# A two-layer graph network: the order of VectorE's and ScalarE's work within one turn of layer 1

## The chip, the cores and the metric

The kernel runs on one core of a Trainium2 chip. The metric is the time of one execution in microseconds of device time. The time before is 8842.36 us, the median of three runs (8837.32 to 8854.7).

## The reference, cut to what matters

12500 nodes have 64 features each; 400000 edges (src, dst) are sorted by dst. Two layers, each with a residual and a layer norm around it. Layer 0 passes every edge's pair of nodes through two small dense layers and sums over dst. Layer 1, to which the change belongs, is a graph attention with four heads:

```
x = (meta_x @ W).reshape(N, HEADS, DIM)
a_src = jnp.sum(x * att_src, axis=-1)
a_dst = jnp.sum(x * att_dst, axis=-1)
logits = leaky_relu(a_src[src] + a_dst[dst], 0.2)       # with a loop edge for each node
seg_max = segment_max(logits, dst)
ex = exp(logits - seg_max[dst])
alpha = ex / (segment_sum(ex, dst) + 1e-16)
msg = x[src] * alpha[:, :, None]
out = segment_sum(msg, dst).mean(axis=1) + bias
```

## The kernel before, in words

Edges are taken in groups of 1024 (8 tiles of 128; an edge is a partition). 8 groups are a superstep; there are 392 groups in 49 supersteps. Nodes lie in 98 blocks of 128. As edges are sorted by dst, a group touches one or two neighbouring blocks. A *turn* works on one group and one block; there are 392 + 97 = 489 turns in a layer. Every engine runs the same two nested loops (`steps`, line 250): over the groups of a superstep, and within one over the blocks of the group, the range of which it loads from a table `Bt` (line 256). Around them, `supers` goes over the supersteps; the start of one takes VectorE through `maxima` (lines 618 to 656), which makes a running maximum of the logits per node with scans.

GpSimd gathers the rows of the source nodes (64 features, a one and the four `a_src`) from DRAM into `big`, one DMA for each 128 edges, into two halves of a superstep each. It waits until the turns that read the old rows have written their Y (semaphore `y1`).

A turn is a pipeline over up to four turns. `k.has(n)` and `k.after(stage, n)` speak of the turn n before the present one. For turn t in layer 1:

- VectorE makes `rel` (dst less the block's first node, line 482) and from it `S`, the one-hot of 1024 edges x 128 nodes in bf16 (line 485). Both are in `onehot`, line 480.
- TensorE transposes S (line 970), ScalarE copies the transposes to `ST` (line 1174), TensorE looks up `a_dst` of the edges with it (line 979, stage `ad`).
- In the next turn, VectorE sums up the lookup (`adx`, 692), adds it to the logits and to the maxima (`zz`, 704 and 705), takes the leaky relu (`lz`, 713) and the difference (`dw`, 722). ScalarE takes the exp into the weights `wb` (line 1178, stage `w`).
- In the turn after, VectorE multiplies the gathered rows by the weights into `Y`, in two halves of 4 tiles (`weigh`, line 665, stages `y0` and `y1`). ScalarE copies in the last columns of Y and an f32 copy of S, `Sf`, half by half (`ends`, lines 1148 and 1149, stages `sf0` and `sf1`). TensorE sums Y over the edges of each node (`sums`, line 956, stages `U0` and `U1`) into one of two banks of `pu`. Its own order in a turn is: sums of half 0, transposes, sums of half 1, lookup. The half-0 sums wait for `tm` of the turn that used the bank before.
- One turn later, VectorE makes the new maximum of the nodes in small steps (`nz`, 700, to `dd`, 728 and 729). ScalarE takes the exp of dd into `ee` (1161), copies the maximum (1163), and makes `Tm`, the new sums scaled, in four steps (1167). VectorE scales the accumulator by ee (stage `old`, line 739), and in the following turn adds Tm to it (stage `acc`, line 684).

The order of each engine's work is written by hand. VectorE's in a turn is: Y half 0, acc, adx with the small chains zz to dw and nz to dd woven into each other, rel, S, Y half 1, old. ScalarE's is: ends of half 1, ee, Tm, ends of half 0, ST, exp of the weights. The end of a turn holds `push`, which shifts registers with the places of earlier turns (line 208). Semaphores carry every dependence.

Of the kernel before, what the change touches and what calls it, by code (L numbers as in the profile page):

```python
# [24 lines left out]
P = 128  # L25
NB = -(-N // P)
LAST = N - (NB - 1) * P
TG = 8
# [30 lines left out]
def build(nc, x, src, dst, W1, b1, W2, b2, W, att_src, att_dst, bias, out, q_dram, x_dram, srcT_dram,  # L59
# [5 lines left out]
    with ctx:  # L65
# [3 lines left out]
        def sem(name):  # L69
# [98 lines left out]
                 "az1": 0, "h0": 1, "h1": 1, "htp": 1, "hts": 1, "z2": 1, "az2": 1,  # L168
                 "h2": 2, "hi": 2, "rest": 2, "mid": 2, "lo": 3, "U": 3, "us": 4, "acc": 4},
                {"rel": 0, "S": 0, "stp": 0, "sts": 0, "ad": 0, "adx": 1, "zz": 1,  # L170
                 "lz": 1, "dw": 1, "w": 1, "sf0": 1, "sf1": 2, "y0": 2, "y1": 2, "U0": 2, "U1": 2, "nz": 3,
                 "nl": 3, "np": 3, "mnew": 3, "dd": 3, "e": 3, "mb": 3, "tm": 3, "old": 3, "acc": 4}]
        L = [{n: sem(f"l{l}_{n}") for n in LAGS[l]} for l in range(2)]

        class Turn:
# [216 lines left out]
        def _(dve):  # L392
# [3 lines left out]
            def link(ins):  # L396

                count[0] += 1
                ins.then_inc(vch, 1)
                dve.wait_ge(vch, count[0])  # L400
# [76 lines left out]
            def hv(ap, h):  # L477
                return ap[:, h * 4:(h + 1) * 4, :]

            def onehot(k, half, buf):  # L480
                k.after("S", 1)
                v.tensor_scalar(rel[:, :], dstc[:, half, ds(k.r * TG, TG)], blk[:, ds(k.b, 1)], None,  # L482
                                ALU.subtract).then_inc(L[k.l]["rel"], 1)
                k.after("rel", 0)
                v.tensor_tensor(S[:, ds(buf, TG), :], iotas[k.l][:, :].unsqueeze(1).to_broadcast([P, TG, P]),  # L485
                                rel[:, :].unsqueeze(2).to_broadcast([P, TG, P]),
                                ALU.is_equal).then_inc(L[k.l]["S"], 1)
# [4 lines left out]
            def turn0(half):  # L492
                m = L[0]

                def turn(k):
                    if k.has(4):
                        k.after("U", 4)
                        k.after("acc", 5)
                        v.tensor_reduce(usum[:, :], ps[6][:, 0:BF].rearrange("p (k d) -> p d k", k=3),
                                        AX.X, ALU.add).then_inc(m["us"], 1)  # L500
                    if k.has(3):
                        k.after("mid", 3)
                        v.tensor_tensor(h2p[:, 2, :], h2, h2p[:, 1, :], ALU.subtract).then_inc(m["lo"], 1)
                    if k.has(0):
                        onehot(k, half, (k.sn % 4) * TG)
                    elif k.has(3):
                        k.after("lo", 3)
                    if k.has(4):
                        b = blocks.back(4 - max(k.tail, 0))
                        k.after("us", 4)  # L510
                        v.tensor_tensor(x0[:, ds(b, 1), :], x0[:, ds(b, 1), :], usum[:, :].unsqueeze(1),
                                        ALU.add).then_inc(m["acc"], 1)
                    if k.has(1):
                        for h in range(2):
                            k.after(f"az{h}", 1)
                            v.tensor_tensor(hv(h1, h), ps[4 + h][:, 0:256].rearrange("p (t d) -> p t d", d=D),
                                            hv(az1, h), ALU.max).then_inc(m[f"h{h}"], 1)
                    if k.has(2):
                        k.after("az2", 2)
                        v.tensor_tensor(h2, ps[7][:, :], az2, ALU.max).then_inc(m["h2"], 1)  # L520
                        k.after("hi", 2)
                        v.tensor_tensor(h2, h2, h2p[:, 0, :], ALU.subtract).then_inc(m["rest"], 1)  # L522
                    if k.has(0):
                        blocks.push(k.b)
                return turn
# [84 lines left out]
            link(v.memset(warm[:, :], 0.0))  # L610
            link(v.memset(wb[:, :, :], 0.0))
            link(v.memset(Tm[:, :, :], 0.0))
            prime(dve, 1, "rel S adx zz lz dw y0 y1 nz nl np mnew dd old acc")
            dve.sem_inc(clean, 1)

# [54 lines left out]
            def turn1(half):  # L670
                m = L[1]

                def turn(k):
                    t = max(k.tail, 0)
                    if k.has(2):
                        at = tiles.back(2 - t)
                        k.after("w", 2)
                        weigh(k, 0, at)
                    if k.has(4):

                        ab = acc[:, ds(blocks1.back(4 - t), 1), :, :].rearrange("p b h d -> p (b h) d")
                        k.after("old", 4)
                        k.after("tm", 4)
                        v.tensor_tensor(ab, ab, Tm[:, :, :], ALU.add).then_inc(m["acc"], 1)  # L684

                    if k.has(1):
                        here = tiles.back(1)
                        zf = zz[:, :, :, :].rearrange("p a t h -> p (a t h)")  # L690
                        k.after("ad", 1)
                        v.tensor_reduce(adx[:, :, :],
                                        ps[2][:, 0:TG * 3 * H].rearrange("p (t k h) -> p t h k", k=3, h=H),
                                        AX.X, ALU.add).then_inc(m["adx"], 1)
                    if k.has(3):
                        b = blocks1.back(3 - t)
                        mb = Mx[:, ds(b, 1), :]
                        ends = pu[:, ds(((k.sn + 1) % 2) * 512, YW)]
                        k.after("U1", 3)
                        v.tensor_tensor(nz[:, 0:1, :], ends[:, UW:UW + H].unsqueeze(1), adst[:, ds(b, 1), :],  # L700
                                        ALU.add).then_inc(m["nz"], 1)
# [26 lines left out]
                        v.tensor_tensor(dd[:, 0:1, :], mb, mnew[:, :].unsqueeze(1), ALU.subtract)  # L728
                        v.tensor_tensor(dd[:, 1, :], nz[:, 2, :], mnew[:, :], ALU.subtract).then_inc(m["dd"], 1)  # L729

                    if k.has(0):
                        k.after("sf1", 2)
                        onehot(k, half, (k.sn % 2) * TG)
                    if k.has(2):
                        weigh(k, 1, at)
                    if k.has(3):
                        ab = acc[:, ds(b, 1), :, :].rearrange("p b h d -> p (b h) d")
                        k.after("e", 3)
                        v.tensor_tensor(ab, ab, ee[:, 0, :].unsqueeze(2).to_broadcast([P, H, D + 1]), ALU.mult
                                        ).then_inc(m["old"], 1)  # L740
                    if k.has(0):
                        tiles.push(k.r * TG + half * TS)
                        blocks1.push(k.b)
# [272 lines left out]
        def _(act):  # L1016
# [121 lines left out]
                    a_.copy(xT[c % 2][:, us[0] * P:(us[-1] + 1) * P], ps[4 + h][:, 0:len(us) * P]  # L1138
                            ).then_inc(tab1["tc"], 1)

            act_tiles = Past(act, "act_tile", 2, 2 * TS - TG)
            act_blocks = Past(act, "act_block", 3, NB - 1)

            def ends(k, h, back):

                k.after(f"U{h}", back + 1)
                at = act_tiles.back(back - max(k.tail, 0))
                a_.copy(Y[:, h * 4:h * 4 + 4, UW:YW], edgeE[:, ds(at + h * 4, 4), :])
                a_.copy(Sf[:, h * 4:h * 4 + 4, :], S[:, ds(((k.sn + back) % 2) * TG + 4 * h, 4), :]  # L1149
                        ).then_inc(L[1][f"sf{h}"], 1)  # L1150

            def turn1(half):
                m = L[1]

                def turn(k):
                    if k.has(2):
                        ends(k, 1, 2)
                    if k.has(3):

                        k.after("dd", 3)  # L1160
                        a_.activation(ee[:, :, :], dd[:, :, :], ACT.Exp).then_inc(m["e"], 1)  # L1161
                        b = act_blocks.back(3 - max(k.tail, 0))
                        a_.copy(Mx[:, ds(b, 1), :], mnew[:, :].unsqueeze(1)).then_inc(m["mb"], 1)
                    if k.has(3):
                        k.after("e", 3)
                        for h in range(H):
                            a = a_.activation(Tm[:, h, :], pu[:, ds(((k.sn + 1) % 2) * 512 + h * (D + 1), D + 1)],
                                              ACT.Copy, scale=ee[:, 1, h:h + 1])
                        a.then_inc(m["tm"], 1)
                    if k.has(1):  # L1170
                        ends(k, 0, 1)
                    if k.has(0):
                        k.after("stp", 0)
                        a_.copy(ST[:, :, :], ps[0][:, :].bitcast(bf16).rearrange("p (t n) -> p t n", t=TG)  # L1174
                                ).then_inc(m["sts"], 1)
                    if k.has(1):
                        k.after("y1", 2)
                        a_.activation(wb[:, :, :], dw[:, :, :], ACT.Exp).then_inc(m["w"], 1)  # L1178
                    if k.has(0):
                        act_tiles.push(k.r * TG + half * TS)  # L1180
                        act_blocks.push(k.b)
                return turn
# [53 lines left out]
```

## Time and profile before

| | |
|---|---|
| median of three runs | 8842.36 us |
| the profiled execution | 8853.59 us, span 8851.8 us |
| granted TensorE clock, mean | 0.888 |
| VectorE busy | 5775.0 us, 65% |
| GpSimd busy | 6098.9 us, 69% |
| TensorE busy (matmul) | 5979.6 us, 68% |
| ScalarE busy | 3918.0 us, 44% |

Layer 0 fills the span to about 3.9 ms, layer 1 from about 4.3 to 8.7 ms. From 4500 to 8500 us VectorE is busy 3075.88 of 4000 us, GpSimd 2816.14, TensorE 2600.49 and ScalarE 1720.59. An engine's busy time leaves out what its sequencer does by itself: register work, branches, waits. "issue" as the end of an idle time means that the engine waited for nothing that the profile shows.

### The profile page before, as it was taken

The numbers are of one execution on the slowest core, as the hardware profiler recorded it, in microseconds if no ns is written. First come the engines' busy times: TensorE is split into PE (matmuls) and PEld (weight loads), VectorE is DVE, ScalarE is ACT, GpSimd is POOL, SyncE is SP. The second block draws the span as 40 slices with busy tenths as digits, with TensorE's granted clock in tenths as the row PEclk, the third lists the DMA queues.
The fourth block names the chain that finished last, engine by engine and source line by source line (L and its number), as shares of the span: only waits on it lengthen the run. The fifth ranks groups of instructions, "written<-read, shape, count | busy, mean of one in ns | idle before, by whom it ended". The sixth has DMA issues, their size and how long they took to land.

```text
span 8851.8 us, 202989 instructions
## 1 busy us (share of the span) xinstructions
PE 5979.6 (68%) x46823; PEld 4612.0 (52%) x46824; DVE 5775.0 (65%) x13889; ACT 3918.0 (44%) x10077; POOL 6098.9 (69%) x6281
## 2 busy tenths in 40 slices
PE   4777777777777777776366666666666666666667
PEld 3556555555555555555244445444444444444446
DVE  3555555555555555556477777777777777777776
ACT  3445444544444444444244444444444444444443
POOL 4777777777777777772777776767676766766650
PEclk7889888988988888888698989999898989999897
DMA  3111111111111111112111111111111111111110
GB/s 99 40 40 40 39 40 40 40 40 40 39 40 40 40 40 40 40 40 30 27 29 30 28 28 26 28 27 28 27 27 27 27 28 26 27 28 27 27 21 15
DMA packets 276883, 301.80 MB, mean 34 GB/s; under 512 B 169511, under 2 KB 173108, under 8 KB 276566
## 3 DMA queue, kind: packets, MB, share of 16 engines
q0 software_dynamic: 200704, 265.33, 14.7%
q1 hardware_dynamic: 74082, 32.92, 1.5%
q10 hardware_dynamic: 2068, 3.20, 0.1%
q8 instruction: 13, 0.21, 0.0%
q14 instruction: 16, 0.13, 0.0%
HBM read 286.33 MB, written 16.30 MB: 34 GB/s over the span
## 4 chain that ended last, share of the span: by engine, by line
DVE 25%; issue 22%; POOL 21%; PE 18%; DVEq 6%; ACT 4%; ACTq 2%; POOLq 1%; DMA 1%; SPq 0%
POOL big L382 21%; DVE S L485 8%; PE ps L970 6%; PE pu L956 4%; DVE state L684 2%; DVE rel L482 2%; PE ps L846 2%; DVE rowA L633 1%; DVE rowD L638 1%; POOLq L373 1%; DVE Y L665 1%; DVEq L256 1%; DVEq L700 1%; ACT rowX L1087 1%; ACT ST L1174 1%
## 5 line engine op out<-in xcount | busy, mean ns | idle before, releaser
L382 POOL DMA_INDIRECT big<-x_dram,idx x3136 | 3084.8, 984 | 1442.5 <-issue 892.7
L382 POOL DMA_INDIRECT big<-q_dram,idx x3136 | 3013.0, 961 | 1041.2 <-issue 1033.9
L956 PE MATMUL pu<-Y,S 128*128 128x265 f32 x7856 | 2147.5, 418 | 738.2 <-DVE Y L665 732.5
L956 PEld LDWEIGHTS pu<-Y,S 128*128 128x128 f32 x7856 | 1497.5, 201 | 1030.8 <-issue 782.2
L665 DVE TENSOR_TENSOR Y<-big,ps 128x1040 f32<-128x1040 f32 x982 | 1210.7, 1233 | 659.0 <-ACT ps L1178 572.5
L485 DVE TENSOR_TENSOR S<-ps,rel 128x1024 f32 x978 | 1197.8, 1225 | 222.1 <-DVE rel L482 222.1
L1075 ACT COPY ST<-ps 128x512 bf16<-128x512 bf16 x978 | 538.8, 586 | 1703.7 <-PE ps L846 1703.6
L860 PE MATMUL pu<-rowX,S 128*128 128x192 bf16 x3936 | 578.0, 264 | 980.4 <-issue 718.6
L522 DVE TENSOR_TENSOR Y<-Y,rowX 128x512 f32<-128x512 f32 x491 | 341.7, 696 | 1221.3 <-ACT rowX L1087 1218.9
L860 PEld LDWEIGHTS pu<-rowX,S 128*128 x3936 | 383.7, 98 | 1174.7 <-issue 1063.5
L970 PE MATMUL ps<-identb,S 128*128 128x128 bf16 x3912 | 550.3, 231 | 523.9 <-DVE S L485 522.7
L970 PEld LDWEIGHTS ps<-identb,S 128*128 x3912 | 375.6, 96 | 838.3 <-issue 727.2
L1161 ACT ACTIVATE ee<-dd 128x8 f32<-128x8 f32 x492 | 102.6, 209 | 1412.6 <-DVE dd L729 1412.6
L1174 ACT COPY ST<-ps 128x1024 bf16<-128x1024 bf16 x489 | 494.9, 1012 | 515.0 <-PE ps L970 511.6
L846 PE MATMUL ps<-identb,S 128*128 128x128 bf16 x3912 | 551.3, 234 | 159.5 <-DVE S L485 152.8
L1149 ACT CAST S<-S 128x512 f32 x981 | 617.4, 629 | 14.1
L883 PE MATMUL ps<-state,ST 128*128 x11736 | 570.3, 199 | 0.0
L893 PE MATMUL pu<-edgeE,rowA 128*128 128x128 f32 x3920 | 567.6, 288 | 0.8 <-ACT rowA L1090 0.8
L883 PEld LDWEIGHTS ps<-state,ST 128*128 128x128 bf16 x11736 | 537.5, 102 | 45.4
L846 PEld LDWEIGHTS ps<-identb,S 128*128 x3912 | 376.0, 97 | 344.3 <-issue 235.9
L893 PEld LDWEIGHTS pu<-edgeE,rowA 128*128 128x128 f32 x3920 | 474.3, 191 | 113.3 <-issue 112.2
L878 PE MATMUL ps<-big,identb 128*128 x2934 | 529.8, 294 | 0.0
(176 smaller groups left out, 8322.6 us busy)
## 6 DMA issues: line engine op xcount, KB each, us to landing
big<-q_dram,idx POOLq DMA_INDIRECT x3136
big<-x_dram,idx POOLq DMA_INDIRECT x3136
rowD<-dst_dram SPq DMA_DIRECT2D x196, 32.0 KB
x_dram<-big SPq DMA_DIRECT2D x7, 483.0 KB, 6.1
idx<-srcT_dram SPq DMA_DIRECT2D x98, 32.0 KB, 1.7
dstc<-dstT_dram SPq DMA_DIRECT2D x98, 32.0 KB
q_dram<-state SPq DMA_DIRECT2D x2, 1536.0 KB, 9.6
out<-big SPq DMA_DIRECT2D x6, 448.0 KB
```

The lines of the kernel that those rows point to most:

```text
L382: nc.gpsimd.indirect_dma_start(o, None, x_dram if l else q_dram, bass.IndirectOffsetOnAxis(ap=idx[:, half, t:t + 1], axis=0)).then_inc(gat ...
L485: v.tensor_tensor(S[:, ds(buf, TG), :], iotas[k.l][:, :].unsqueeze(1).to_broadcast([P, TG, P]), rel[:, :].unsqueeze(2).to_broadcast([P, TG ...
L665: v.tensor_tensor(Y[:, rows, 0:UW].rearrange("p t (h d) -> p t h d", h=H), g1[:, ds(at + h * 4, 4), 0:D + 1].unsqueeze(2).to_broadcast([P, ...
L846: last = t_.transpose(o[:, t * P:t * P + P], hot[:, h * 4 + t, :], identb[:, :])
L860: last = t_.matmul(ps[6][:, 0:BF].rearrange("p (k d) -> p k d", k=3), hot[:, t, :], h2p[:, :, t * D:t * D + D], start=(t == 0), stop=(t == ...
L883: last = t_.matmul(ps[4 + h][:, t * D:t * D + D], ST[:, h * 4 + t, :], pq[:, 0, ds(k.b, 1), j, :], start=False, stop=(t == 3 and j == 2), ...
L893: last = t_.matmul(ps[7][:, j * P:j * P + P], h1T[:, j, :], w2d[:, :], start=False, stop=(j == 3), skip_group_check=True)
L956: last = t_.matmul(bank, Sf[:, t, :], Y[:, t, :], start=(t == 0), stop=(t == 7))
L970: last = t_.transpose(o[:, t * P:t * P + P], hot[:, t, :], identb[:, :])
L1075: a_.copy(ST[:, h * 4:h * 4 + 4, :], ps[h][:, 0:2 * P].bitcast(bf16).rearrange("p (t n) -> p t n", t=4)).then_inc(L[k.l][f"sts{h}"], 1)
L1149: a_.copy(Sf[:, h * 4:h * 4 + 4, :], S[:, ds(((k.sn + back) % 2) * TG + 4 * h, 4), :]).then_inc(L[1][f"sf{h}"], 1)
L1174: a_.copy(ST[:, :, :], ps[0][:, :].bitcast(bf16).rearrange("p (t n) -> p t n", t=TG)).then_inc(m["sts"], 1)
```

## The change

VectorE's turn in layer 1 is put in another order: rel, Y half 0, S, Y half 1, old, adx, acc, then the woven small chains. `onehot` is split into `places` (rel) and `onehot` (S). The scaling of the accumulator (`old`) goes one turn later, so that it stands in the same turn as acc, two instructions ahead of it. ScalarE's turn is put in the order: ends of half 0, ST, exp of the weights, ends of half 1 (now for the turn one back and not two), ee, the copy of the maximum, Tm. `ee` is set to one ahead of layer 1. TensorE's and GpSimd's programs are the same.

```diff
-                 "lz": 1, "dw": 1, "w": 1, "sf0": 1, "sf1": 2, "y0": 2, "y1": 2, "U0": 2, "U1": 2, "nz": 3,
-                 "nl": 3, "np": 3, "mnew": 3, "dd": 3, "e": 3, "mb": 3, "tm": 3, "old": 3, "acc": 4}]
+                 "lz": 1, "dw": 1, "w": 1, "sf0": 1, "sf1": 1, "y0": 2, "y1": 2, "U0": 2, "U1": 2, "nz": 3,
+                 "nl": 3, "np": 3, "mnew": 3, "dd": 3, "e": 3, "mb": 3, "tm": 3, "old": 4, "acc": 4}]
...
-            def onehot(k, half, buf):
+            def places(k, half):
                 k.after("S", 1)
                 v.tensor_scalar(rel[:, :], ...).then_inc(L[k.l]["rel"], 1)
+
+            def onehot(k, buf):
                 k.after("rel", 0)
                 v.tensor_tensor(S[:, ds(buf, TG), :], ...).then_inc(L[k.l]["S"], 1)
...
                 def turn(k):                                   # VectorE, layer 1
                     t = max(k.tail, 0)
+                    if k.has(0):
+                        places(k, half)
                     if k.has(2):
                         at = tiles.back(2 - t)
                         k.after("w", 2)
                         weigh(k, 0, at)
+                    if k.has(0):
+                        k.after("sf1", 2)
+                        onehot(k, (k.sn % 2) * TG)
+                    if k.has(2):
+                        weigh(k, 1, at)
                     if k.has(4):
-
                         ab = acc[:, ds(blocks1.back(4 - t), 1), :, :].rearrange("p b h d -> p (b h) d")
-                        k.after("old", 4)
-                        k.after("tm", 4)
-                        v.tensor_tensor(ab, ab, Tm[:, :, :], ALU.add).then_inc(m["acc"], 1)
+                        k.after("e", 4)
+                        v.tensor_tensor(ab, ab, ee[:, 0, :].unsqueeze(2).to_broadcast([P, H, D + 1]), ALU.mult
+                                        ).then_inc(m["old"], 1)
...                                                              # adx
+                    if k.has(4):
+                        k.after("old", 4)
+                        k.after("tm", 4)
+                        v.tensor_tensor(ab, ab, Tm[:, :, :], ALU.add).then_inc(m["acc"], 1)
...                                                              # nz, zz, ... dd; then, before:
-                    if k.has(0):
-                        k.after("sf1", 2)
-                        onehot(k, half, (k.sn % 2) * TG)
-                    if k.has(2):
-                        weigh(k, 1, at)
-                    if k.has(3):
-                        ab = acc[:, ds(b, 1), :, :].rearrange("p b h d -> p (b h) d")
-                        k.after("e", 3)
-                        v.tensor_tensor(ab, ab, ee[:, 0, :].unsqueeze(2).to_broadcast([P, H, D + 1]), ALU.mult
-                                        ).then_inc(m["old"], 1)
...
                 def turn(k):                                   # ScalarE, layer 1
-                    if k.has(2):
-                        ends(k, 1, 2)
+                    if k.has(1):
+                        ends(k, 0)
+                    if k.has(0):
+                        k.after("stp", 0)
+                        a_.copy(ST[:, :, :], ...).then_inc(m["sts"], 1)
+                    if k.has(1):
+                        k.after("dw", 1)
+                        k.after("y1", 2)
+                        a_.activation(wb[:, :, :], dw[:, :, :], ACT.Exp).then_inc(m["w"], 1)
+                        ends(k, 1)
                     if k.has(3):
                         k.after("dd", 3)
                         ...                                      # ee, Mx, Tm
-                    if k.has(1):
-                        ends(k, 0, 1)
-                    if k.has(0):
-                        k.after("stp", 0)
-                        a_.copy(ST[:, :, :], ...).then_inc(m["sts"], 1)
-                    if k.has(1):
-                        k.after("y1", 2)
-                        a_.activation(wb[:, :, :], dw[:, :, :], ACT.Exp).then_inc(m["w"], 1)
```

## Rows read from the trace of the kernel before

**Rows 1.** Waits, 4700 to 8600 us: who for whom, total, times, longest.
```profile
DVE Y L665 <- ACT ps L1178: 505.6, 390, 1.4
...
POOL big L382 <- DVE Y L665: 381.9, 207, 10.0
...
DVE rowA L633 <- PE ps L938: 55.7, 43, 2.3
```

**Rows 2.** Groups by line, VectorE, 4700 to 8600 us: busy, mean ns, idle before.
```profile
L485 DVE TENSOR_TENSOR S<-ps,rel 128x1024 f32 x432 | 529.1, 1225 | 97.8 <-DVE rel L482 97.8
```

**Rows 3.** Page, part 5, the one-hots of both layers.
```profile
L485 DVE TENSOR_TENSOR S<-ps,rel 128x1024 f32 x978 | 1197.8, 1225 | 222.1 <-DVE rel L482 222.1
```

**Rows 4.** Instructions of line 253 (the loop over groups): min/median/max ns.
```profile
L253 DVEq FUSED_REGOPS  x784: 81/199/229, 88.4 to 8707.6; - x196
```

**Rows 5.** Timeline of one layer-1 turn on VectorE: start, duration.
```profile
6005.09 0.23 DVE L482 TENSOR_SCALAR rel<-dstc,blk 128x8 bf16 x1
...
6005.54 1.22 DVE L485 TENSOR_TENSOR S<-ps,rel 128x1024 f32 x1 [0.22 <-DVE rel L482]
...
6006.69 1.23 DVE L665 TENSOR_TENSOR Y<-big,ps 128x1040 f32<-128x1040 f32 x1
...
6007.83 0.42 DVE L739 TENSOR_TENSOR state<-state,ee 128x260 f32 x1
...
6009.54 1.24 DVE L665 TENSOR_TENSOR Y<-big,ps 128x1040 f32<-128x1040 f32 x1 [1.29 <-ACT ps L1178]
...
6010.70 0.42 DVE L684 TENSOR_TENSOR state<-state,Tm 128x260 f32 x1
...
6011.20 0.15 DVE L700 TENSOR_TENSOR nz<-pu,adst 128x4 f32 x1
...
6012.56 0.16 DVE L729 TENSOR_TENSOR dd<-nz,mnew 128x4 f32<-128x4 f32 x1
...
6013.16 1.22 DVE L485 TENSOR_TENSOR S<-ps,rel 128x1024 f32 x1 [0.22 <-DVE rel L482]
```

**Rows 6.** Waits of VectorE in layer 0, 300 to 3900 us.
```profile
DVE Tm L499 <- issue: 450.6, 354, 1.9
```

**Rows 7.** Timeline, VectorE, layer 0: a turn's end and the next one's start.
```profile
2010.13 0.69 DVE L522 TENSOR_TENSOR Y<-Y,rowX 128x512 f32<-128x512 f32 x1 [1.20 <-ACT rowX L1087]
2010.76 0.36 DVE L499 TENSOR_REDUCE Tm<-pu 128x64 f32<-128x192 f32 x1
```

**Rows 8.** Timeline, VectorE, a superstep's maxima and the turn behind them.
```profile
6015.78 0.60 DVE L626 COPY edgeA<-big 128x64 f32<-128x64 f32 x4
...
6018.86 1.21 DVE L633 TENSOR_TENSOR_SCAN rowA<-rowX,ps 32x512 f32<-32x512 f32 x1 [0.64 <-PE ps L938]
...
6027.89 0.28 DVE L654 TENSOR_SCALAR edgeE<-ps 128x64 f32<-128x64 f32 x1
...
6029.93 1.24 DVE L665 TENSOR_TENSOR Y<-big,ps 128x1040 f32<-128x1040 f32 x1 [1.76 <-issue]
...
6033.62 1.23 DVE L485 TENSOR_TENSOR S<-ps,rel 128x1024 f32 x1 [0.23 <-DVE rel L482]
```

**Rows 9.** Timeline, TensorE and ScalarE behind the same maxima.
```profile
6031.51 3.52 PE L956 MATMUL pu<-Y,S 128*128 128x265 f32 x8 [5.12 <-DVE Y L665]
...
6035.10 1.14 PE L970 MATMUL ps<-identb,S 128*128 128x128 bf16 x8
...
6036.14 2.03 PE L956 MATMUL pu<-Y,S 128*128 128x265 f32 x8
...
6038.56 0.62 ACT L1149 CAST S<-S 128x512 f32 x1
...
6040.83 0.21 ACT L1161 ACTIVATE ee<-dd 128x8 f32<-128x8 f32 x1 [1.66 <-DVE dd L729]
...
6041.22 0.94 ACT L1167 ACTIVATE Tm<-pu,ee 128x65 f32 x4
```

**Rows 10.** Windows: that turn; PE, PEld, DVE, ACT, POOL busy, granted clock.
```profile
6029.93:6037.63 7.70, 6.06 (x23) 4.55 (x24) 6.01 (x17) 3.09 (x10) 5.69 (x6) 0.70 0.19 40
```

More of the change, by code:

```diff
@@ L504, in turn @@
                     if k.has(0):
-                        onehot(k, half, (k.sn % 4) * TG)
+                        places(k, half)
+                        onehot(k, (k.sn % 4) * TG)
                     elif k.has(3):
@@ L612, in _ @@
             link(v.memset(Tm[:, :, :], 0.0))
+            link(v.memset(ee[:, :, :], 1.0))
             prime(dve, 1, "rel S adx zz lz dw y0 y1 nz nl np mnew dd old acc")
@@ L674, in turn @@
                     t = max(k.tail, 0)
+                    if k.has(0):
+                        places(k, half)
                     if k.has(2):
@@ L1139, in _, with ends @@
                             ).then_inc(tab1["tc"], 1)
-            act_tiles = Past(act, "act_tile", 2, 2 * TS - TG)
+            act_tiles = Past(act, "act_tile", 1, 2 * TS - TG)
             act_blocks = Past(act, "act_block", 3, NB - 1)
-            def ends(k, h, back):
-                k.after(f"U{h}", back + 1)
-                at = act_tiles.back(back - max(k.tail, 0))
+            def ends(k, h):
+                k.after(f"U{h}", 2)
+                at = act_tiles.back(1 - max(k.tail, 0))
                 a_.copy(Y[:, h * 4:h * 4 + 4, UW:YW], edgeE[:, ds(at + h * 4, 4), :])
-                a_.copy(Sf[:, h * 4:h * 4 + 4, :], S[:, ds(((k.sn + back) % 2) * TG + 4 * h, 4), :]
+                a_.copy(Sf[:, h * 4:h * 4 + 4, :], S[:, ds(((k.sn + 1) % 2) * TG + 4 * h, 4), :]
                         ).then_inc(L[1][f"sf{h}"], 1)
@@ L1155, in turn @@
                 def turn(k):
-                    if k.has(2):
-                        ends(k, 1, 2)
+                    if k.has(1):
+                        ends(k, 0)
+                    if k.has(0):
+                        k.after("stp", 0)
+                        a_.copy(ST[:, :, :], ps[0][:, :].bitcast(bf16).rearrange("p (t n) -> p t n", t=TG)
+                                ).then_inc(m["sts"], 1)
+                    if k.has(1):
[3 more added lines that the diff above has]
+                        ends(k, 1)
                     if k.has(3):
@@ L1163, in turn @@
                         a_.copy(Mx[:, ds(b, 1), :], mnew[:, :].unsqueeze(1)).then_inc(m["mb"], 1)
-                    if k.has(3):
                         k.after("e", 3)
@@ L1169, in turn @@
                         a.then_inc(m["tm"], 1)
-                    if k.has(1):
-                        ends(k, 0, 1)
-                    if k.has(0):
-                        k.after("stp", 0)
-                        a_.copy(ST[:, :, :], ps[0][:, :].bitcast(bf16).rearrange("p (t n) -> p t n", t=TG)
-                                ).then_inc(m["sts"], 1)
-                    if k.has(1):
-                        k.after("y1", 2)
-                        a_.activation(wb[:, :, :], dw[:, :, :], ACT.Exp).then_inc(m["w"], 1)
                     if k.has(0):
```

## Prediction, made before the changed kernel had run

> **What bounds the kernel now.** The change touches only layer 1's turn, so I read the waits of a stretch that lies wholly in layer 1 (4700 to 8600 us). The reader is to see three of them [rows 1]. VectorE waits for the weights `wb` at line 665: 505.6 us in 390 waits, 1.30 us a turn. GpSimd waits for `Y` (that is, for a free half of `big`) 381.9 us, so the gathers are not the limit, but they have no more than 381.9 of 3900 us, 9.8%, to give. And VectorE waits for TensorE at the first scan of each superstep, 55.7 us in 43.
>
> Then the turn itself in order of time [rows 5]. From one S to the next are 7.62 us, and VectorE stands still in them only before line 665. The loop that sets this length is: S, transposes, copy of the transposed one-hot, exp of the weights behind it, and Y of the next turn.
>
> Counts. Page part 5 has 978 one-hots in two layers, so 489 turns a layer [rows 3]; line 253 ran 784 times, 392 groups a layer [rows 4]. A new group begins with 392 turns, 49 of these a new superstep. So of layer 1's 488 intervals between turns 48 hold the superstep's maxima, 343 cross into a new group ("outer"), and 97 stay in one group and go to another block ("inner"). The interval with the maxima is 20.46 us in one case (6013.16 to 6033.62 [rows 5, 8]); the wait at the scan is 0.64 us there (from what stands between 6015.78 and 6018.86) and 55.7/43 = 1.30 on the mean, so 21.1 us on the mean. From 432 one-hots in 3900 us [rows 2]: (3900 - 43 x 21.1) / 389 = 7.69 us is the mean turn now.
>
> **VectorE's own loop after the change.** New order: rel, Y half 0, S, Y half 1, old, adx, acc, the small chain to dd. I go from start to start [rows 5]:
> - S to Y half 1: 5.54 to 6.69, 1.15. Y half 1 to old: 1.14.
> - old to acc: acc now stands right behind the product it waits for. old takes 0.42, and S starts 0.22 behind the end of rel, on which it waits in the same way. I take 0.57 (between 0.46 and 0.68); adx goes in between and costs nothing.
> - acc to nz: today 0.50 with adx between. I take 0.39; the bounds are 0.34 (the pitch of that 0.42 us instruction alone) and 0.50.
> - nz to the last dd: 11.20 to 12.56, 1.36. Some of it is zz waiting for adx, which now is done earlier: I take 1.26 (1.16 to 1.36).
> - rel to Y half 0: 0.33. Today 0.45 passes from rel to S, with a wait for rel in it that Y hasn't got; below 0.20 it can't go, as rel itself takes that.
> - Y half 0 to S: 1.16, as 9.54 to 10.70.
>
> These are 6.00 us. The wait of 1.30 is gone, and about 0.3 of pauses behind rel and adx. But VectorE's sequencer does the loop's register work and branch, and a load from `Bt` where a new group begins, between the last instruction of a turn and the first of the next. Today this lies beneath the half-1 product, old and the 1.30 wait. In the new order nothing long is ahead of it: the turn ends with instructions of 0.16 us. Layer 0 shows what the work costs bare: its turn ends with line 522 (0.69 us) and starts with line 499, and there VectorE stood 450.6 us in 354 waits for nothing but issue [rows 6], 1.27 each. So an outer boundary is 0.69 + 1.27 = 1.96 from start to start. An inner one has 0.63 (2010.13 to 2010.76, at most that, as line 522 covers it) [rows 7]. At a superstep's start, which lacks the branch, 1.76 us lie between the end of line 654 (6028.17) and line 665 [rows 8]. I take 1.95 outer (1.80 to 2.15) and 0.83 inner (0.63 to 1.05), as layer 1's turn has some more registers. So outer 7.95 us, inner 6.83 us, mean (343 x 7.95 + 97 x 6.83) / 440 = 7.70. That is today's turn: **the wait is traded for the loop's control**, one for one.
>
> A rule weighed against these rows. In layer 0 line 522 waits 1.20 us for ScalarE, and the turn's control work doesn't use that wait: line 499 still comes 1.27 us late [rows 6, 7]. So here the sequencer stays with a waiting instruction. The Trainium skill (Perfetto Trace Analysis, Per-engine timelines) says that an instruction of VectorE is pushed into a wait queue and that the sequencer is then ready for the next. By that rule the boundary could begin before the last dependent steps of the small chain are released, VectorE's loop would be some 0.2 us shorter (7.50), and the sum below 8 us lower. I go by the rows.
>
> **The loop that the new order closes through ScalarE and TensorE.** TensorE's half-0 sums wait for `tm` of the turn before, as the bank of `pu` is used again. ScalarE now makes Tm behind `ends` of half 1, and that waits for U1, the end of TensorE's half-1 sums. So: sums 0, transposes, sums 1, edge columns and Sf, ee, Tm, and sums 0 again, all of it once in each turn. The superstep's first turn shows TensorE's part back to back [rows 9]. With sums 0 at 2.03 (as at 6036.14): to the transposes 0.07 (6035.03 to 6035.10), to sums 1 1.04, to their end 2.03, to the CAST of Sf 0.39 (6038.17 to 6038.56), to ee 0.52 (the 0.62 of the CAST less the usual overlap of 0.1), to Tm 0.39 (6040.83 to 6041.22), to its end 0.94, and to sums 0 0.39, an estimate (one release and two instructions of the sequencer, each near 0.1; 0.2 to 0.5). Sum 2.03 + 0.07 + 1.04 + 2.03 + 0.39 + 0.52 + 0.39 + 0.94 + 0.39 = 7.80 us. Today Tm is made between the two `ends`, right behind dd, and this loop isn't closed.
>
> 7.80 is above VectorE's mean of 7.70. An outer turn of VectorE (7.95) is a bit slower than the loop and an inner one (6.83) much faster: TensorE falls behind by a microsecond in an inner turn and makes up 0.15 in each outer one. VectorE feels it through sf1, for which the one-hot waits: Sf half 1 is ready 0.39 + 0.62 behind the end of sums 1, and S can start about 0.3 later. With sums 0 starting 1.91 into VectorE's turn (Y half 0 ends at 0.33 + 1.24, and 0.34 for the release, as 6031.17 to 6031.51 [rows 8, 9]), sf1 lets S of the next turn go at 1.91 + 5.17 + 1.01 + 0.3 = 8.39, against 7.95 + 1.49 = 9.44 in an outer turn and 8.32 in an inner one. So in an outer turn TensorE may be nearly 1.1 late, in an inner one not at all: each inner turn is stretched from 6.83 to about 7.4, and the mean is 7.82, just over the loop's 7.80. (7.82 - 7.69) x 440 = **+57 us**.
>
> After each superstep's maxima TensorE runs its first sums at the lower of its two clocks, 1.2 GHz: 3.52 us instead of 2.03, in a turn with a mean granted clock of 0.70 [rows 9, 10]. Today this costs next to nothing (that turn is 7.70). In the new loop the 1.49 us exceed the margin of 1.1 by 0.4: x 48 = **+20 us**.
>
> **The interval with the maxima.** S to Y 1 to old to acc to nz to dd: 1.15 + 1.14 + 0.57 + 0.39 + 1.26 = 4.51. To line 626: the leaving branches without the load, 0.70 (an estimate between the inner and the outer boundary). Line 626 to the scan: today 3.08 [rows 8], with 0.64 of waiting for TensorE's last sums; these now end earlier against VectorE, so 2.44 and 0.2 for late ones. From the scan (6018.86) to the end of line 654 9.31 as now. To rel 1.76, to Y 0.33, to S 1.16. Sum 20.4 against 21.1, 0.7 x 48 = **-34 us**.
>
> All else is small: one memset more before layer 1, ScalarE's old Tm path off VectorE's back, the last four turns (unrolled, no control). Copies into `ST` are early enough for the weights: exp ends near 6.5 in a turn, and Y needs it beyond 7.
>
> **Sum.** 57 + 20 - 34 = +43 us on the profiled execution's 8853.6 us (span 8851.8 and 1.8 around it): 8897. The median of the runs shown is 8842.4, 11.2 lower, so 8886 us on its scale.
>
> **Rivals.**
> 1. *Only VectorE's loop counts* (the path through ScalarE and TensorE is shorter than 7.70, for instance as sums 0 go sooner behind tm). For it: it hangs on nine small steps, 0.1 us off the sum suffices. Then 0.01 x 440 + no clock cost, and 0.9 x 48 off the maxima: -39, 8803 us. Chance 0.20.
> 2. *The whole wait comes back* (control hidden after all, and that loop short). 1.30 us x 440 and more; GpSimd then limits it to 9.8% of layer 1's 440 x 7.69 + 48 x 21.1 = 4396 us: 430 us, about 8412. Against: rows 6. Chance 0.05.
> 3. *No change*: wait and control cancel, and the closed loop costs what the maxima give back: 8842, within 10. Chance 0.14.
> 4. *Slower by VectorE itself*: the small steps at their upper bounds (0.68, 0.50, 1.36, 0.45, boundary 2.15 and 1.05), 6.44 + control: outer 8.59, inner 7.49, mean 8.35 at the very worst; half way, 8.03, is what I price: 0.34 x 440 + 20 - 34 = +136, 8978 us. It decides from a mean of 7.82 on. Chance 0.13.
> 5. Forecast, turn 7.75 to 7.95, 8855 to 8945 us: 0.48.
>
> What a measurement of this kernel can tell from no change is about 0.2%, 18 us. Faster: rivals 1 and 2 and a little of the others, 0.27. Same: 0.15. Slower: 0.58. Range 8785 to 8960: it takes in rival 1 and the better part of rival 4.
>
> **What would show it.** The idle time of VectorE before Y half 0 (line 665's successor) with ScalarE as its end goes to near zero, and a new idle time with "issue" as its end stands before rel, 1.7 us in most turns: if it is under 1, my boundary is wrong. The half-0 sums should be released by Tm of ScalarE, not by Y: if they are released by Y throughout, the closed loop is wrong and rival 1 holds. Inner turns should be 7.3 to 7.5, outer ones 7.9 to 8.0, and the first turn of a superstep about 8.3. The scan's wait for TensorE should fall from 1.3 to some 0.2. A time under 8780 would mean that control work is not on the path at all.

## Result and the profile after

The changed kernel takes 8817.05 us, the median of 7 runs (8809.5 to 8836.08), against 8842.36 of before (7 runs, 8833.76 to 8854.7): a ratio of 0.9971, 95% interval 0.996 to 0.9982. It is faster by 0.3% (25 us), where 43 us slower were forecast. A second comparison gave 8821.72 against 8845.82, ratio 0.9972 (0.996 to 0.9983). The profiled execution of after took 8836.08 us (span 8834.3), the slowest of its seven, and lies 17.5 below that of before.

The waits between 4700 and 8600 us, after. They answer to [rows 1], with the columns of these.

```profile
ACT Y L1149 <- PE pu L957: 2231.3, 869, 16.9
...
PE pu L957 <- DVE Y L669: 821.4, 254, 5.3
...
DVE rel L482 <- issue: 624.5, 435, 1.7
PE pu L957 <- ACT Tm L1175: 411.6, 180, 2.3
POOL big L382 <- DVE Y L669: 303.6, 92, 10.1
...
DVE S L487 <- ACT S L1150: 46.1, 55, 1.2
...
DVE Y L669 <- ACT ps L1166: 19.8, 22, 1.7
```

VectorE's 505.6 us of waiting for the weights are now 19.8. In their place stand 624.5 us before rel, 1.44 a turn, ended by nothing but issue: the loop's control. And TensorE waits for Tm 180 times, which it did not do before. The first was forecast (1.7 in most turns); the second only in part, as Tm was to release the half-0 sums in every turn, and in 254 turns Y still does.

One outer turn on VectorE, after, in order of time; it answers to [rows 5].

```profile
6002.81 0.42 DVE L693 TENSOR_TENSOR state<-state,ee 128x260 f32 x1
...
6003.32 0.42 DVE L705 TENSOR_TENSOR state<-state,Tm 128x260 f32 x1
6003.66 0.16 DVE L711 TENSOR_TENSOR nz<-pu,adst 128x4 f32 x1
...
6005.05 0.16 DVE L740 TENSOR_TENSOR dd<-nz,mnew 128x4 f32<-128x4 f32 x1
...
6006.94 0.23 DVE L482 TENSOR_SCALAR rel<-dstc,blk 128x8 bf16 x1 [1.74 <-issue]
6007.26 1.24 DVE L669 TENSOR_TENSOR Y<-big,ps 128x1040 f32<-128x1040 f32 x1
...
6008.42 1.22 DVE L487 TENSOR_TENSOR S<-ps,rel 128x1024 f32 x1
...
6009.55 1.23 DVE L669 TENSOR_TENSOR Y<-big,ps 128x1040 f32<-128x1040 f32 x1
...
6010.69 0.42 DVE L693 TENSOR_TENSOR state<-state,ee 128x260 f32 x1
```

From old to old are 7.88 us: old to acc 0.51, to nz 0.34, to dd 1.39, control to rel 1.89, to Y 0.32, then 1.16, 1.13 and 1.14.

From all starts of S in layer 1, in us (the number of intervals ahead):

| | before | after | forecast |
|---|---|---|---|
| 343 outer | 7.68 | 7.89 | 7.9 to 8.0 |
| 97 inner | 7.70 | 7.15 | about 7.4 |
| these 440 | 7.68 | 7.72 | 7.86 (7.82, and 0.4 in each first turn) |
| of them the 48 behind the maxima | 7.68 | 8.36 | 8.35 |
| 48 with the maxima in between | 21.10 | 20.44 | 20.4 |

So the turns cost 0.042 x 440 = +18 us and the maxima gave 0.66 x 48 = -32 us: -13 of the 17.5. Of the profiles' remaining 4 us, 8 lie behind the last one-hot (137.7 us before, 129.7 after) and 4 the other way ahead of the first. The 8 look like chance: the second profile of after has 134.0 there, and other kernels of this study, with the same closing stage, 132.3 to 142.2.

TensorE's clock fell: a mean granted clock of 0.91 before and 0.87 after, in the windows 4470 to 8470 us (us, PE, PEld, DVE, ACT, POOL busy, clock, DMA share, GB/s). Before:

```profile
4470.00:8470.00 4000.00, 2591.86 (x15236) 1951.67 (x15235) 3075.37 (x8289) 1714.99 (x5374) 2822.01 (x2868) 0.91 0.15 28
```

After:

```profile
4470.00:8470.00 4000.00, 2422.11 (x15282) 1940.08 (x15283) 3074.24 (x8312) 1680.04 (x5391) 2858.40 (x2875) 0.87 0.16 28
```

Turns whose half-0 sums last over 2.2 us are 64 of 441 before, 166 after. In both kernels 48 of these stand behind the maxima, so away from them such sums went from 16 to 118. Over the slow sums of after the granted clock is 0.61 on the mean (0.5 of full speed is the lower of its two levels, 1.2 GHz), over the others 1.00. This I had not forecast beyond the turn behind the maxima. Timeline of TensorE and ScalarE, after, a slow sum and, in the next turn, the loop at full clock; the latter answers to [rows 9].

```profile
6008.80 3.01 PE L957 MATMUL pu<-Y,S 128*128 128x265 f32 x8 [3.35 <-DVE Y L669]
...
6017.27 2.06 PE L957 MATMUL pu<-Y,S 128*128 128x265 f32 x8 [2.27 <-ACT Tm L1175]
...
6019.16 0.61 PE L971 MATMUL ps<-identb,S 128*128 128x128 bf16 x8
...
6019.61 2.01 PE L957 MATMUL pu<-Y,S 128*128 128x265 f32 x8
...
6021.89 0.62 ACT L1150 CAST S<-S 128x512 f32 x1
6022.42 0.20 ACT L1170 ACTIVATE ee<-dd 128x8 f32<-128x8 f32 x1
...
6022.75 0.93 ACT L1175 ACTIVATE Tm<-pu,ee 128x65 f32 x4
```

The slow sums shown follow 3.35 us in which TensorE had stood still (new order: Y half 0 comes only behind VectorE's control). Away from the maxima, 74 of the 109 half-0 sums that followed 3 us or more of standing still were slow, and 32 of the 294 that followed less than 2.5 us. In the other piece, sums 0 to transposes take 1.89, to sums 1 0.45, to their end 2.01, to Tm's end 2.06; with 0.40 to the next sums it is 6.81 us. That is the median of the 107 turns whose half-0 sums were released by Tm with both sums at full clock; in the 166 with slow sums the median loop is 8.48. The transposes have a part in this: queued behind the sums they take 0.45 us at the high clock and 0.85 at the lower one.

How that reaches VectorE can be read from its own steps. In a turn that waits for nothing, S comes 1.16 us behind Y half 0, and Y half 0 0.32 behind rel; the means over the 440 turns are 1.30 and 0.37. These two waits, for Sf of half 1 (0.15) and for the weights (0.05), are nearly all of what the mean turn of 7.72 has above the 7.51 of the turns without a wait; the other six steps are within 0.02 of their undisturbed length.

### The profile page after: what moved, and what is told of

Same layout as the page of the kernel before. It is cut to its first block, busy times and chain, and to the rows that moved or that the text cites. A ratio compares the mean times of both kernels' runs of the same rounds, so it can differ in the third digit from the quotient of the medians.

```text
span 8834.3 us, 202985 instructions
## 1 busy us (share of the span) xinstructions
PE 5775.2 (65%) x46823; PEld 4581.8 (52%) x46824; DVE 5761.4 (65%) x13891; ACT 3873.4 (44%) x10075; POOL 6131.4 (69%) x6281
## 4 chain that ended last, share of the span: by engine, by line
DVE 23%; PE 21%; POOL 21%; issue 21%; DVEq 7%; ACT 4%; POOLq 1%; ACTq 1%; DMA 1%; SPq 0%
POOL big L382 21%; PE pu L957 12%; DVE Y L669 6%; DVE S L487 3%; DVEq L256 2%; PE ps L847 2%; PE ps L971 2%; DVE rowA L637 1%; DVE rowD L642 1%; ACT Tm L1175 1%; DVE state L693 1%; POOLq L373 1%; DVEq L253 1%; ACT rowX L1088 1%; PE pu L861 1%
## 5 line engine op out<-in xcount | busy, mean ns | idle before, releaser
L957 PE MATMUL pu<-Y,S 128*128 128x265 f32 x7856 | 2267.2, 436 | 1394.4 <-DVE Y L669 926.2
L957 PEld LDWEIGHTS pu<-Y,S 128*128 128x128 f32 x7856 | 1582.4, 212 | 1704.1 <-issue 1433.8
L1149 ACT COPY Y<-edgeE 128x20 f32 x980 | 205.1, 209 | 2516.9 <-PE pu L957 2516.9
L482 DVE TENSOR_SCALAR rel<-dstc,blk 128x8 bf16 x978 | 249.9, 255 | 704.5 <-issue 704.5
L847 PE MATMUL ps<-identb,S 128*128 128x128 bf16 x3912 | 553.0, 234 | 160.6 <-DVE S L487 153.0
L847 PEld LDWEIGHTS ps<-identb,S 128*128 x3912 | 376.8, 97 | 346.7 <-issue 237.7
L501 DVE TENSOR_REDUCE Tm<-pu 128x64 f32<-128x192 f32 x493 | 176.4, 358 | 499.6 <-issue 497.1
```

The costliest lines, as they stand in the source:

```text
L847: last = t_.transpose(o[:, t * P:t * P + P], hot[:, h * 4 + t, :], identb[:, :])
L957: last = t_.matmul(bank, Sf[:, t, :], Y[:, t, :], start=(t == 0), stop=(t == 7))
```

## Experiments

All times are medians of 4 to 11 runs, the ratio is to the kernel before on the same chip. Some comparisons came to chips on which all kernels took half as long again; these stand last.

**1 and 2. Is control bare at the end of VectorE's turn, and was it hidden before?** One more load of a register, which nothing uses, in both kernels.

```diff
                     if k.has(0):
+                        dve.value_load(Bt[0:1, AHEAD:AHEAD + 1], min_val=0, max_val=NB - 1)
                         tiles.push(k.r * TG + half * TS)
```

> The changed kernel, with one more register load of VectorE's sequencer from the table Bt at the end of each layer-1 turn; its value isn't used. The loop's own load shows as 0.30 us. Theory A and B both say that control stands bare at the end of VectorE's turn now: 0.35 us x 489 = +170 us, less where a turn waits for Sf anyway: 8940 to 8995 us. Rival (control runs beneath the last instructions): 8817 us, no change.

> The kernel before, with the same additional register load at the end of each layer-1 turn of VectorE. My prediction had it that control is hidden there, beneath the half-1 product, old and the wait for the weights: no change, 8835 to 8855 us. Rival (control is on the path there too): +170 us, 9010 us.

After with it: 9106.49 us, ratio 1.029 (1.0275 to 1.0304), 289 us above after, 0.59 us a turn (289 / 489). Before with it: 8849.92, ratio 1.0002 (0.9993 to 1.0011). The same load costs nothing in one order and 289 us in the other. I had expected 0.35 a turn, and 8940 to 8995 us; the time lies above that. The wait of VectorE before rel in the load's kernel, 4700 to 8600 us:

```profile
DVE rel L482 <- issue: 828.2, 409, 2.4
```

2.02 us a turn against 1.44: the 0.58 lie where they should.

**3. The loop through Tm opened.** ScalarE's `ends(k, 1)` put behind Tm, in the changed kernel.

> The changed kernel, with one thing moved: ScalarE makes ee, the copy of the maximum and Tm ahead of the edge columns and Sf of half 1. TensorE's half-0 sums then no longer hang on the end of the half-1 sums of the turn before. Theory A (the closed loop ScalarE/TensorE, made long by TensorE's lower clock in 166 of 441 turns, stretches VectorE's turns from 7.52 to 7.72 us): the wait of TensorE for Tm (411.6 us between 4700 and 8600 us) goes, the mean turn falls to 7.5 to 7.65 us, time 8735 to 8790 us. Sf of half 1 comes later, so that inner turns may wait for it; that takes some of the gain. Theory B (VectorE's own work and its control set the time, TensorE's waits are only idle time): 8805 to 8830 us, as the changed kernel.

8862.72 us, ratio 1.0012 (1.0002 to 1.0021): slower than after (0.9971), and above what either theory allowed. TensorE's wait for Tm is gone (no turn is released by it) and nothing is won. The mean turn is 7.77, the wait of the one-hot for Sf rose from 46.1 to 60.6 us, and 207 turns have slow sums instead of 166. The waits, 4700 to 8600 us:

```profile
PE pu L957 <- DVE Y L669: 1080.7, 415, 5.3
...
DVE S L487 <- ACT S L1150: 60.6, 87, 1.3
```

So theory A, that opening this loop frees VectorE, failed in this form: the edit lengthens another path while it opens this one. The half-1 Sf is ready 1.74 us behind the half-1 sums (median), where it was 0.90, and TensorE, released by Y alone, still starts from a standstill.

**4 and 5. Small matmuls that keep TensorE busy while its sequencer goes round.** 24, and 48, at the end of TensorE's layer-1 turn of the changed kernel; nothing uses their result.

```diff
                     last.then_inc(L[1]["ad"], 1)
+                    for t in range(24):
+                        t_.matmul(ps[4][:, 0:P], identb[:, :], identb[:, :], start=True, stop=True)
```

> The changed kernel, with 24 more small matmuls of TensorE at the end of each layer-1 turn (identity by identity into an unused bank), which fill the 3 us in which it now stands still while its sequencer goes round the loop and Y is made. Nothing waits for them. Theory A: the sums of half 0 run at 2.05 us nearly always (now over 2.2 us in 166 of 441 turns), the loop falls to 6.8 us, the mean turn to VectorE's own 7.5 to 7.6, time 8735 to 8770 us. Theory B (the lower clock falls in idle time and costs nothing): 8805 to 8850 us, a little slower if the small matmuls get in the way.

> The changed kernel with 48 small matmuls, again. 8765 to 8785 us if 48 clear most of the slow sums, 8790 to 8830 us if they delay the sums.

24: 8787.98 us, ratio 0.9927 (0.9913 to 0.9941), faster than after's 0.9972, but short of the 8735 to 8770 that theory A gave. Slow sums fell from 166 to 96 turns, the mean turn from 7.72 to 7.59, the turns behind the maxima from 8.36 to 8.01. What VectorE's turn has above 7.51 fell from 0.21 to 0.08 us, nearly all of it at the two waits for Sf and the weights. TensorE waits 136.2 us for Tm, instead of 411.6 (4700 to 8600 us):

```profile
PE pu L957 <- DVE Y L669: 632.4, 294, 5.6
...
PE pu L957 <- ACT Tm L1177: 136.2, 146, 1.0
```

48: 9070.15 us, ratio 1.0254 (1.024 to 1.0268). That is 240 us above the higher of my two ranges. Slow sums 49, the turn is 8.06 and the interval with the maxima 22.17: the added matmuls now stand in the way, as TensorE waits for issue ahead of its sums:

```profile
PE pu L957 <- issue: 274.0, 289, 1.0
```

**6. The same 24 in the kernel before.**

> The kernel before with 24 small matmuls, again. Theory A: 8835 to 8855 us, no change; rival (a warm TensorE helps either kernel alike): 8815 us or less. On the slow chip the added instructions of TensorE cost 2%.

8879.97 us, ratio 1.0039 (1.0025 to 1.0053): slower by 34 us, where I had expected no change, 8835 to 8855. The turn stays at 7.67, though the slow sums fell from 64 to 48, all of them behind the maxima; the interval with the maxima went from 21.10 to 21.79, 0.69 x 48 = 33 us. VectorE's scan there waits longer for TensorE (85.3 us between 4700 and 8600 us, 55.7 before), which has the added matmuls ahead of it. Here fewer slow sums bring nothing, as they are not in the loop.

**7. Control put beneath a long instruction.** The changed kernel; VectorE's turn ends with Y half 0 of the group one back.

```diff
-                 "dw": 1, "w": 1, "sf0": 1, "sf1": 1, "y0": 2,
+                 "dw": 1, "w": 1, "sf0": 1, "sf1": 1, "y0": 1,
...
-                k.after(f"U{h}", 3)
+                k.after(f"U{h}", 2 + h)
...
-                    if k.has(2):
-                        at = tiles.back(2 - t)
-                        k.after("w", 2)
-                        weigh(k, 0, at)
...                                          # behind dd, last in the turn:
+                    if k.has(1):
+                        k.after("w", 1)
+                        weigh(k, 0, here)
```

> The kernel `rotate` again, since the chip of its first run took 13550 us for the kernel before and says nothing of 8842. Expected as then: theory A 8500 to 8640 us; theory B (the loop ScalarE/TensorE alone sets the time) 8780 to 8820 us.

**8605.8 us**, ratio 0.9733 (0.972 to 0.9746), within the 8500 to 8640 of theory A: faster than both kernels, 2.4% below after. The mean turn is 7.21 (outer 7.42, inner 6.47). VectorE, end of an outer turn and start of the next:

```profile
6004.88 1.24 DVE L669 TENSOR_TENSOR Y<-big,ps 128x1040 f32<-128x1040 f32 x1
6006.03 0.36 DVE L482 TENSOR_SCALAR rel<-dstc,blk 128x8 bf16 x1
6006.62 1.23 DVE L487 TENSOR_TENSOR S<-ps,rel 128x1024 f32 x1 [0.22 <-DVE rel L482]
```

Its waits, VectorE's and then TensorE's, 4700 to 8600 us:

```profile
DVE rel L482 <- issue: 284.3, 355, 2.0
DVE Y L669 <- ACT ps L1165: 167.2, 170, 2.7
```

```profile
PE pu L956 <- ACT Tm L1174: 915.0, 401, 2.3
```

Idle time before rel fell from 624.5 to 284.3 us. Now TensorE's half-0 sums are released by Tm nearly every time: the closed loop that I had forecast for the change is the limit here, 6.81 us at full clock (309 turns), 8.48 with slow sums (83 turns; behind the maxima left out).

The edit also lets TensorE start its half-0 sums earlier, so it could have helped by that alone. But VectorE's own turn got shorter too: outer turns without a wait take 7.06 and 6.84 us in the two copies of the loop, where after has 7.87 and 7.65, 0.81 less. The mean fell by only 0.5, as the waits for the weights grew.

**8. After again.**

> The changed kernel again, on a chip of the usual speed: 8817 us, within 15; from the last one-hot to the end 129 to 143 us.

8821.72 us (8810.54 to 8824.99), slow sums 171 of 441, mean turn 7.69: as the first time.

**9 to 11. Only on slow chips.** `rotate` with 24 matmuls, `rotate` with Tm ahead of `ends(k, 1)`, and after with 12 matmuls, twice each.

> The kernel `rotate` (8606 us) with 24 small matmuls at the end of TensorE's layer-1 turn. In `rotate` the half-0 sums are released by Tm in each turn; the loop ScalarE/TensorE takes 6.8 us at full clock and 8.5 us in the 103 turns of 412 whose half-0 sums run at the lower clock. Theory A (the lower clock is what stretches): slow sums fall below 60, mean turn 7.21 to 7.0, time 8520 to 8560 us. Rival (the stretch comes from the loop's length at any clock): 8595 to 8620 us.

> `rotate` with 24 small matmuls again; the first time the chip took 13543 us for the kernel before. Theory A (the lower clock is what stretches): 8520 to 8560 us on a chip where the kernel before takes 8845. Rival (the loop's length at any clock): 8595 to 8620 us.

> The kernel `rotate` with ScalarE's ee, maximum and Tm ahead of the edge columns and Sf of half 1. It opens the loop through Tm, in which TensorE waited in every turn. In the changed kernel the same move gained nothing (8863 against 8817 us). If the loop through Sf (sums 1, Tm, Sf of half 1, one-hot) is as tight: 8600 to 8680 us. If Tm was what counts: mean turn 6.9 to 7.0, 8480 to 8540 us.

> `rotate` with Tm ahead of the edge columns and Sf of half 1, again. If the loop through Sf is as tight as the one through Tm: 8600 to 8680 us; if Tm was what counts: 8480 to 8540 us.

> The changed kernel with 12 small matmuls. 24 gave 8788 us with 96 slow sums of 441, 48 gave 9070 as they got in the way. Theory A (what counts is how many half-0 sums are slow): between, 130 or so slow sums and 8795 to 8810 us. Rival (the gain of 24 comes from something else, as the place of the code in memory): no such order, 8780 or below, or 8817 and above.

> The changed kernel with 12 small matmuls, again. Theory A: 8795 to 8810 us and about 130 slow half-0 sums of 441; rival: 8780 or below, or 8817 and above.

The kernel before took 13543 and 13210 us there. The ratios were 0.9993 and 1.0045 for the first, 0.9854 and 0.9901 for the second, 0.9886 and 0.9964 for the third. Experiments 5 to 8 had also come to such a chip first (before 13550 us):

> The changed kernel with VectorE's turn put so that it ends with a long instruction: rel, S, Y half 1, old, adx, acc, the small chains, and then Y half 0 of the group one back, whose weights ScalarE has by then. The 1.8 us of loop control then run beneath the 1.15 us of that product. Theory A (control bare at the turn's end is what ate the wait): VectorE's own turn falls from 7.52 us to about 6.85 (1.15 less in outer turns, 0.15 to 0.3 back for S behind rel), if TensorE keeps its clock; with the loop ScalarE/TensorE at 6.8 (full clock) to 8.5 us (low clock) the mean turn is 7.0 to 7.3, time 8500 to 8640 us. Theory B (the loop ScalarE/TensorE alone sets the time): 8780 to 8820 us.

> The changed kernel once more, on the chip of these comparisons: 8817 us, within 15. The stretch from the last one-hot to the end was 129.7 us in its first profile against 137.7 before, which no step of mine explains; if it is chance (the clock of TensorE in the closing phase) it lies anywhere from 129 to 143 us here.

> The kernel before with the same 24 small matmuls at the end of TensorE's layer-1 turn that took the changed kernel from 8817 to 8788 us. Before, the half-0 sums are slow in 64 of 441 turns only, and TensorE isn't in the loop that sets the turn's length but for the transposes. Theory A: 8835 to 8855 us, no change; rival (a warm TensorE helps either kernel alike): 8815 us or less.

> The changed kernel with 48 small matmuls instead of 24. If 24 leave slow sums (96 turns of 441) because they end too early, 48 clear most of these: mean turn 7.52 to 7.56, time 8765 to 8785 us. If they reach into the time when Y is ready they delay the half-0 sums: 8790 to 8830 us.

Ratios: `rotate` 0.9911, after 0.9836, before with 24 matmuls 1.019, after with 48 1.0197. TensorE stands still up to 30 us there, its weight loads waiting for nothing that the profile shows, and the others wait for it; why is not known. In after's profile from 6000 to 11000 us:

```profile
PEld ps L980 <- issue: 1610.4, 219, 30.5
PE ps L980 <- ACT ST L1161: 1540.6, 122, 30.1
```

None of these tells the theories of 8842 us apart, so the rival that the expectation of `warm12` names, that 24 matmuls gained by something other than the clock, was not tested by a run on a chip of the usual speed. That after beat before there too, and more clearly, holds; that `rotate` is 2.4% better than after does not hold there.

## Why the prediction was wrong, step by step

The time is 69 us below the forecast of 8886. On the profiles it is 61, and 59 of these lie in the 440 turns (+57 and +20 forecast, +18 measured). Two terms of the sum were too long, and what the lower clock costs away from the maxima was missing, which hid a part of that.

- **The wait is traded for control: right.** The wait for the weights went, 1.44 us of issue a turn came, and experiments 1, 2 and 7 show it from three sides.
- **The loop through ScalarE and TensorE, 7.80: there, but not of that length. This is the step that made a slower kernel of it**, as it stood as a floor under every turn. It is 6.81 at full clock. I took 1.04 us for the transposes from a turn in which TensorE was waiting for S and got them one by one [rows 9]; queued behind the sums they take 0.45. They also start 1.89 us behind the start of the sums, not 2.10. The CAST behind U1 and Tm behind ee came 0.12 and 0.06 sooner. So 7.80 was no floor under the turn, and "7.82, just over the loop's 7.80" was false: measured are 7.72 with the turns behind the maxima, where I had 7.86. Inner turns, which that loop was to stretch to 7.4, take 7.15.
- **VectorE's own loop, 7.70: mis-sized too.** Turns without a wait show 7.51: outer 7.87 in even and 7.65 in odd supersteps (counted from 0; each has its own copy of the turn's code), inner 6.73 and 6.52. The terms: acc 0.51 behind old, not 0.57; nz 0.34, its bound below, not 0.39; outer control 1.89 and 1.78 in the two copies, not 1.95; inner control about 0.75 and 0.65, not 0.83. One went the other way: nz to the last dd takes 1.38 and 1.27, not 1.26, the first of them above my upper bound of 1.36. Together 0.19 too much, x 440 = 84 us. Put right alone it would have left the forecast slower, as the floor of 7.80 stood above it. With 7.51 and 6.81 the sum is (7.51 - 7.68) x 440 - 32 = -107 us.
- **What stretches the turn from 7.51 to 7.72** is a cause that I named only for the turn behind the maxima: TensorE at its lower clock after it stood still, in 166 turns. That its clock takes part is shown by 24 matmuls in the changed kernel (-0.13 us a turn, at the waits for Sf and the weights) and by the same in before (no change of the turn). That it is all isn't shown. Nor did moving Tm ahead of Sf help: that lengthens the path through Sf.
- **Turns behind the maxima**: 8.35 forecast, 8.36 in the first profile of after and 8.17 in the second. That is partly luck: the outer turn beneath was put at 7.95 and is 7.76, the stretch at 0.4 and is 0.4 to 0.6. **The interval with the maxima**, 20.4 and 20.44: right.
- The first rival (8803 us) came nearest, and for its reason, a loop through TensorE shorter than 7.70 at full clock. But it held VectorE's loop at 7.70 and had no stretch: two errors that cancel in part.
- The rule on the wait queue (the Trainium skill, Perfetto Trace Analysis, Per-engine timelines), by which a waiting instruction doesn't hold the sequencer, again didn't show. In all 489 turns of after the first control record stands 0.01 to 0.02 us behind the start of L739, the last instruction of the chain that waits for a semaphore, and not ahead of it. The 7.50 that the prediction worked out by that rule is near the 7.51 measured, but for other reasons, those of the terms above.

The sum as it should have been: (7.51 + 0.21 - 7.68) x 440 = +18, and -32, together -14 us of 8854.

## What to carry to other kernels

VectorE's loop control (registers, branch, a load) lay beneath whatever long instruction was issued last before it, and bare behind short ones: let a turn end with a long instruction that nothing later in the turn needs, not with small dependent ones; here that was worth 2.4%. When a reordering removes a wait, ask first what else had been running under that wait. A sum of steps whose result is the difference of two nearly equal loops needs each step to 0.02 us; where rows don't give that, the forecast is "no change", with both signs.

## What the runs showed of the hardware

Eight transposes take 1.02 to 1.04 us when TensorE was standing still and waiting for their input (before, 436 turns) and 0.45 us when they are queued behind sums (after, 356 turns), both at a granted clock of 1.0; queued at 0.5 they take 0.85. One register load with its checks is 0.59 us of a bare turn, twice its 0.30 us row. Eight of TensorE's sums took 2.05 us at the high clock and up to 3.90 at the lower one. 24 matmuls that nobody needs, put where TensorE had stood still, cut the turns with sums over 2.2 us from 166 to 96 and made the changed kernel 0.4% faster; in the kernel before they cost 0.4%. Two copies of the same loop body differed by 0.21 us a turn, half of it in the control and half in the small chain; why is not known. The first control record of VectorE's turn stood 0.01 to 0.02 us behind the start of the last instruction that waited for a semaphore, in all 489 turns of after.
